# Self-attention on TensorE: a double unit from value products to scores, and new places for the projections

## The chip, the core and the metric

The kernel runs on one core of one Trainium2 chip. The metric is the time of one execution on the device, in microseconds; the median of several runs is compared. The core has TensorE (matmuls, transposes), ScalarE, VectorE, GpSimd and SyncE (starts DMAs). Each works through its own list of instructions in order, and they wait for each other by semaphores. The tables call them PE (its weight loads: PEld), ACT, DVE, POOL and SP.

## The reference, cut to what matters

After an adapter (a first attention over a short context) come a self-attention, a cross-attention and a feed-forward, each with a residual, for 4 batches of 512 tokens and 160 features. The change is in the self-attention:

```python
DIM, HEADS, DHEAD = (160, 20, 64)
def cross_attention(x, ctx, wq, wk, wv, wo, bo):          # here ctx is layer_norm(x) too
    q = jnp.einsum('bne,ef->bnf', x, wq).reshape(B, N, HEADS, DHEAD).transpose(0, 2, 1, 3)
    ...
    scores = jnp.einsum('bhnd,bhmd->bhnm', q, k) * SCALE
    attn = jax.nn.softmax(scores, axis=-1)
    out = jnp.einsum('bhnm,bhmd->bhnd', attn, v)
    out = out.transpose(0, 2, 1, 3).reshape(B, N, HEADS * DHEAD)
    return jnp.einsum('bnf,fe->bne', out, wo) + bo
x = cross_attention(layer_norm(x, g1, be1), layer_norm(x, g1, be1), wq1, wk1, wv1, wo1, bo1) + x
```

## The kernel before

The 20 heads are taken as 10 pairs (`j`), and a pair as 4 units (`u = 4j + q`): the scores of 128 tokens against all 512, for both heads. A batch has `NU` = 40 units. The loop over a batch is written out over `d` from 0 to 19, a *double unit* each (units `2d` and `2d + 1`); the loop over batches is a hardware loop for the first three, and a last body without a next batch. What is ahead of the current batch's end is taken from the next batch by `over`.

What is done for a pair or unit, with the letters used here:

- **Q, K, V** (`project`): the projections of pair `j`, all into one PSUM bank, `b_proj`. ScalarE copies or rounds the bank; for q and k VectorE then writes the rest (value minus rounded value), L558 and L562. The bank is free for the next projection after that; for V after ScalarE's copy, L486. Scores use q and k as rounded part and rest.
- **S** (`scores`, L380): scores of two units, each into its own pair of banks. Then for each unit VectorE takes the negated maxima (L566), ScalarE two exponentials with sums (L494), VectorE the reciprocals (L570, `inverses`), and GpSimd scales the probabilities in place (L633).
- **T** (`turns`, L394): eight transposes of one unit's probabilities into the two banks `b_turn`, one for each head. VectorE copies the first bank (L575), ScalarE the second (L505). A T waits for the copies of the T before it.
- **W** (`pv`, L407): value products of two units, from the copies and v. After a pair's last one ScalarE copies the result (`copy_att`, L500).

The scores run `LEAD` = 2 double units ahead: d begins with the scores of units `2d + 4` and `2d + 5`. Then follow W of units `2d - 2` and `2d - 1`, T(2d), a projection, T(2d + 1), and in even d one more. So TensorE's order is S W T V T Q in even d and S W T K T in odd d; V, Q and K of d are for pair `d // 2 + 2`.

Between these lies the layer norm of the next batch, or of the next block: statistics (L131, L135) at the end of d = 6 and standardizing at the end of d = 7 on VectorE (`LN_AT`), transposes into `b_proj` at the end of d = 11 and 13 (`TURN_MAIN`, `TURN_TAIL`; L157, L164), and from d = 15 (`ROUND_AT`) the rounding on ScalarE (L193 to L196) and the remainders on VectorE (L206, L208). At a batch's end TensorE does the last W and the output projection (L414) into `b_turn`, VectorE adds it to x (L583), and the loop jumps back.

## Time and profile before

| | |
|---|---|
| median of 3 runs | 1208.08 us (1207.51 to 1211.06) |
| profiled execution, its own time | 1205.71 us |
| its span, first to last instruction | 1203.6 us |
| TensorE busy | 1105.7 us, 92% of the span |
| VectorE, ScalarE, GpSimd busy | 57%, 54%, 29% |
| self-attention | about 213 to 886 us of the span |
| mean granted TensorE clock | 0.982 of full speed |

In a timeline a row begins with the start (us from the span's start) and the duration; [0.60 <-DVE ...] is the time that the engine was idle before, and what ended it. A matmul's shown end includes its drain, so a next matmul starts before it; a TensorE gap is therefore read between starts.

### The profile page before, as it was taken

What the parts mean: (1) busy time and instruction counts of PE and PEld (TensorE: products, weight loads), DVE (VectorE), ACT (ScalarE), POOL (GpSimd) and SP (SyncE); (2) the same over time, 40 slices, a digit from 0 to 9 for tenths busy, and PEclk for the clock granted to TensorE, in tenths of its full rate; (3) what the DMA queues carried; (4) which work ended last, traced back from release to release, by engine and by line L of the source; (5) the groups of instructions that cost most, each with busy time, mean ns of one, the idle gap of its engine ahead of it and who ended that gap; (6) DMA issues with size and microseconds to landing.
All of it is one profiled execution on the core that took longest, in us unless ns stands there. A gap on an engine that the chain in (4) does not pass through costs nothing. (4 is left out here: it accounts for less than half of the span.)

```text
span 1203.6 us, 20434 instructions
## 1 busy us (share of the span) xinstructions
PE 1105.7 (92%) x6668; PEld 759.2 (63%) x6668; DVE 684.5 (57%) x1350; ACT 654.6 (54%) x1450; POOL 352.9 (29%) x470
## 2 busy tenths in 40 slices
PE   7999999699999899998999998999889999999898
PEld 3555555465656665656656567656477878786787
DVE  4474564456665466563666644666547575757253
ACT  2543445366676366673666764666616464646242
POOL 2330322234433234331344322343313132312110
PEclk9999999699999999999999999999999999999899
DMA  6400000000000000000000000000120000000000
GB/s 180 103 1 1 0 1 1 0 1 2 1 1 2 2 1 1 1 1 3 1 1 1 1 1 1 1 1 1 39 55 2 1 0 0 0 1 1 1 22 23
DMA packets 17815, 13.69 MB, mean 11 GB/s; under 512 B 8196, under 2 KB 16324, under 8 KB 17732
## 3 DMA queue, kind: packets, MB, share of 16 engines
q1 hardware_dynamic: 17732, 12.60, 4.2%
q8 instruction: 50, 0.82, 0.3%
q14 instruction: 33, 0.27, 0.1%
HBM read 11.29 MB, written 1.31 MB: 10 GB/s over the span
## 5 line engine op out<-in xcount | busy, mean ns | idle before, releaser
L633 POOL TENSOR_SCALAR sa_probs<-sa_probs,sa_inverse 128x512 f32<-128x512 f32 x320 | 220.2, 701 | 408.4 <-DVE sa_inverse L570 408.4
L494 ACT ACTIVATE sa_probs<-banks,sa_negmax 128x512 f32<-128x512 f32 x320 | 217.5, 687 | 131.6 <-DVE sa_negmax L566 131.5
L566 DVE TENSOR_REDUCE sa_negmax<-banks 128x2 f32<-128x1024 f32 x160 | 194.3, 1217 | 83.7 <-PE banks L380 83.2
L394 PEld LDWEIGHTS banks<-ident,sa_probs 128*128 128x128 f32 x1280 | 144.1, 142 | 101.7 <-POOL sa_probs L633 52.7
L394 PE MATMUL banks<-ident,sa_probs 128*128 128x128 f32 x1280 | 173.5, 279 | 29.3 <-POOL sa_probs L633 26.5
L575 DVE COPY sa_turned<-banks 128x512 f32<-128x512 f32 x160 | 110.3, 689 | 89.5 <-PE banks L394 84.8
L380 PE MATMUL banks<-sa_k_parts,sa_q_parts 64*128 64x512 f32 x960 | 135.2, 412 | 22.9 <-DVE sa_k_parts L562 17.2
L407 PE MATMUL banks<-sa_turned,sa_v 128*64 128x512 f32 x640 | 155.2, 605 | 0.1
L505 ACT COPY sa_turned<-banks 128x512 f32<-128x512 f32 x160 | 94.4, 590 | 80.5 <-PE banks L394 80.5
L380 PEld LDWEIGHTS banks<-sa_k_parts,sa_q_parts 64*128 64x128 f32 x960 | 86.3, 187 | 61.3 <-ACT sa_probs L494 21.2
L1503 POOL TENSOR_TENSOR ca_probs<-ca_probs,ca_inverse 128x616 f32<-128x616 f32 x40 | 48.8, 1219 | 159.8 <-DVE ca_inverse L1451 159.8
L407 PEld LDWEIGHTS banks<-sa_turned,sa_v 128*64 128x64 f32 x640 | 38.6, 136 | 74.6 <-issue 72.4
L1383 ACT COPY ca_turned<-banks 77x512 f32<-77x512 f32 x80 | 42.7, 583 | 71.7 <-PE banks L1316 71.7
L1307 PEld LDWEIGHTS banks<-ca_k_diag,ca_q 128*128 128x128 f32 x320 | 44.4, 193 | 34.7 <-DVE ca_v L1432 23.3
L494 ACT ACTIVATION_READ_ACCUMULATOR sa_probs<-banks,sa_negmax 128x1 f32 x320 | 64.4, 201 | 0.0
L1307 PE MATMUL banks<-ca_k_diag,ca_q 128*128 128x154 f32 x320 | 53.1, 310 | 5.6 <-DVE ca_v L1432 3.1
L562 DVE TENSOR_TENSOR sa_k_parts<-banks,sa_k_parts 128x512 fp32r<-128x512 f32 x40 | 27.7, 692 | 49.6 <-ACT sa_k_parts L482 49.6
L1326 PE MATMUL banks<-ca_turned,ca_v 77*64 77x512 f32 x160 | 46.2, 634 | 2.3 <-ACT ca_turned L1383 2.3
L1336 PEld LDWEIGHTS banks<-w_o,ca_att 128*128 128x128 f32 x320 | 45.7, 198 | 4.0 <-issue 4.0
L1336 PE MATMUL banks<-w_o,ca_att 128*128 128x160 f32 x320 | 46.7, 309 | 0.0
L414 PEld LDWEIGHTS banks<-w_o,sa_att 128*128 128x128 f32 x320 | 43.6, 190 | 3.2 <-issue 3.2
L414 PE MATMUL banks<-w_o,sa_att 128*128 128x160 f32 x320 | 44.5, 300 | 0.0
(187 smaller groups left out, 1900.4 us busy)
## 6 DMA issues: line engine op xcount, KB each, us to landing
w_o<-in_L_xattn_wo SPq DMA_DIRECT2D x2, 800.0 KB, 6.7
out<-x SPq DMA_DIRECT2D x4, 320.0 KB, 2.4
x<-in_x SPq DMA_DIRECT2D x1, 960.0 KB, 5.7
ad_raw_main<-in_L_xattn_wq SPq DMA_DIRECT2D x1, 640.0 KB, 4.3
ad_raw_main<-in_L_xattn_wk SPq DMA_DIRECT2D x1, 640.0 KB, 6.3
ad_raw_main<-in_L_xattn_wv SPq DMA_DIRECT2D x1, 640.0 KB, 8.3
raw_main<-in_L_xattn_wq SPq DMA_DIRECT2D x1, 640.0 KB, 4.4
raw_main<-in_L_xattn_w_ff SPq DMA_DIRECT2D x1, 640.0 KB, 4.6
```

The source lines that it names most:

```text
L380: last = pe.matmul(bank[:, e, :], q_parts[rows, j % 2, a, q * P:(q + 1) * P], k_parts[rows, j % 2, c, :], start=(i == 0), stop=(i == 2))
L394: last = pe.transpose(b_turn[e][:, q * P:(q + 1) * P], probs[:, j % 2, e, q, k * P:(k + 1) * P], ident[:])
L407: last = pe.matmul(b_out[e * HD:(e + 1) * HD, :], v[:, V_BUF[j // 2], k, c:c + HD], turned[:, u % 2, e, :], start=(k == 0), stop=(k == QT ...
L414: last = pe.matmul(b_turn[q // 2][:, q % 2 * D:(q % 2 + 1) * D], att[:, j, q * P:(q + 1) * P], w_o[:, j, :], start=(j == 0), stop=(j == NP ...
L494: act.activation(probs[:, j % 2, e, q, :], b_scores[u % 2][:, e, :], ACT.Exp, bias=negmax[:, u % RING, e:e + 1], accum_out=total[:, u % RI ...
L505: act.copy(turned[:, u % 2, 1, :], b_turn[1]).then_inc(s_evac_act.sem, 1)
L566: dve.tensor_reduce(negmax[:, u % RING, :], b_scores[u % 2], AX_X, ALU.max, negate=True).then_inc(s_max.sem, 1)
L575: dve.tensor_copy(turned[:, u % 2, 0, :], b_turn[0]).then_inc(s_evac.sem, 1)
L633: pool.tensor_scalar(probs[:, j % 2, e, q, :], probs[:, j % 2, e, q, :], inverse[:, u % RING, e:e + 1], 1.0, ALU.mult, ALU.mult).then_inc( ...
L1307: last = pe.matmul(b_scores[:, q // 2, (q % 2) * 2 * SK:(q % 2 + 1) * 2 * SK], q_sb[:, j % BUFS, q * P:(q + 1) * P], k_diag[:, j % BUFS, : ...
L1336: last = pe.matmul(b_out[half][:, t * D:(t + 1) * D], att[:, j, q * P:(q + 1) * P], w_o[:, j, :], start=(j == 0), stop=(j == NPAIR - 1))
L1503: pool.tensor_tensor(p, p, inverse[:, j % BUFS, :].unsqueeze(2).broadcast_to([P, 2 * QT, SK]), ALU.mult).then_inc(s_norm.sem, 1)
```

## The change

TensorE's double unit now begins with the value products W and ends with scores, those of units `2d + 6` and `2d + 7` (the third next double unit). The projections have new places: V between W and T(2d) and K between the two T in even d, both for pair `d // 2 + 2`; Q between the two T in odd d, for pair `d // 2 + 3`. V's bank is copied by VectorE instead of ScalarE. ScalarE does both units' exponentials ahead of its copies of T. VectorE takes both maxima first, and issues the reciprocals of the double unit's second unit in the same double unit. The norm's transposes stand between W and T(2d), their scaling between the exponentials; its rounding and remainders stand at the head of d = 15. Ahead of the loop, Q and K of pairs 0 and 1 go into four banks (`b_proj`, `b_out`, `b_turn[0]`, `b_turn[1]`), V of the two follows behind the first scores, and the scores of six units (0 to 5) instead of four are made there, with Q of pair 2.

```diff
@@ TensorE
-            for what in (V, Q, K):
-                project(0, 0, what)
+            ln.ready(pe, 0)
+            project_q(0, 0, b_proj)
+            project_k(0, 0, b_out)
+            project_q(0, 1, b_turn[0])
+            project_k(0, 1, b_turn[1])
             scores(0, 0)
             scores(0, 1)
-            project(0, 1, V)
-            project(0, 1, Q)
-            scores(0, 2)
-            project(0, 1, K)
-            scores(0, 3)
+            project_v(0, 0, b_proj)
+            pe.wait_ge(s_klo.sem, s_klo.at(0, 0))
+            project_v(0, 1, b_out)
+            for u in range(2, 2 * LEAD):
+                scores(0, u)
+            project_q(0, 2, b_turn[0])
+            for u in range(2 * LEAD, 2 * LEAD + 2):
+                scores(0, u)
+            pe.wait_ge(s_qlo.sem, s_qlo.at(0, 2))
 
             def batch(b, more):
                 for d in range(ND):
                     norm, _, nb = following(b, more)
-                    for i in range(2):
-                        over(scores, b, 2 * (d + LEAD) + i, NU, more)
                     if d >= 1:
                         pv(b, 2 * d - 2)
                         pv(b, 2 * d - 1)
-                    turns(b, 2 * d)
...
+                    if d % 2 == 0:
+                        over(next_v, b, d // 2 + 2, NPAIR, more)
                     if d == TURN_MAIN:
                         norm.turn_main(pe, nb, ident, b_proj, lambda: pe.wait_ge(s_klo.sem, s_klo.at(b, d // 2 + 2)))
                     if d == TURN_TAIL:
                         norm.turn_tail(pe, nb, ident, b_proj, lambda: pe.wait_ge(s_klo.sem, s_klo.at(b, d // 2 + 2)))
+                    turns(b, 2 * d)
...
+                    if d % 2 == 0:
+                        over(next_k, b, d // 2 + 2, NPAIR, more)
+                    else:
+                        over(next_q, b, d // 2 + 3, NPAIR, more)
+                    turns(b, 2 * d + 1)
+                    for i in range(2):
+                        over(scores, b, 2 * (d + LEAD + 1) + i, NU, more)
@@ ScalarE
+                    if d == ROUND_AT:
+                        norm.round(act, nb, operands_free(b + 1))
                     over(exps, b, 2 * (d + LEAD), NU, more)
-                    if d % 2 == 0 and d > 0:
-                        copy_att(b, d // 2 - 1)
-                    copy_turned(b, 2 * d)
-                    if d < ND - 1:
-                        over(round_part, b, middle(d)[0], NPAIR, more, middle(d)[1])
-                    over(exps, b, 2 * (d + LEAD) + 1, NU, more)
-                    copy_turned(b, 2 * d + 1)
...
+                    over(exps, b, 2 * (d + LEAD) + 1, NU, more)
+                    if d % 2 == 0 and d > 0:
+                        copy_att(b, d // 2 - 1)
+                    copy_turned(b, 2 * d)
+                    if d % 2 == 0:
+                        over(round_k, b, d // 2 + 2, NPAIR, more)
+                    else:
+                        over(round_q, b, d // 2 + 3, NPAIR, more)
+                    copy_turned(b, 2 * d + 1)
@@ VectorE
+            def copy_v(b, j, bank=b_proj):
+                dve.wait_ge(s_v.sem, s_v.at(b, j))
+                dve.wait_ge(s_pv.sem, s_pv.at(b, 2 * QT * (V_BEFORE[j // 2] + 1) - 1))
+                dve.tensor_copy(v[:, V_BUF[j // 2], j % 2 * 2:j % 2 * 2 + 2, :].rearrange("p a c -> p (a c)"), bank).then_inc(s_vsb.sem, 1)
...
                     over(maxima, b, m, NU, more)
-                    over(inverses, b, m - 1, NU, more)
-                    if d % 2 == 1:
-                        over(rest, b, end(d - 1)[0], NPAIR, more, Q)
-                    if d == ROUND_AT + 1:
+                    if d == ROUND_AT:
                         norm.remainder(dve, nb, operands_free(b + 1))
                     over(maxima, b, m + 1, NU, more)
                     over(inverses, b, m, NU, more)
+                    if d % 2 == 0:
+                        over(copy_v, b, d // 2 + 2, NPAIR, more)
                     copy_turned(b, 2 * d)
-                    if d % 2 == 1 and d < ND - 1:
-                        over(rest, b, middle(d)[0], NPAIR, more, K)
+                    over(inverses, b, m + 1, NU, more)
                     copy_turned(b, 2 * d + 1)
...
+                    if d % 2 == 0:
+                        over(rest_k, b, d // 2 + 2, NPAIR, more)
+                    else:
+                        over(rest_q, b, d // 2 + 3, NPAIR, more)
```

TensorE in d = 2, before. L380 is S (one row for each of its two units), L407 the value products, L394 T, L226 to L229 the first of V's two identical fours, L218 the first of Q's four.

```order
L380 MATMUL banks<-sa_k_parts,sa_q_parts 128x512 x6
...
L380 MATMUL banks<-sa_k_parts,sa_q_parts 128x512 x6
L407 MATMUL banks<-sa_turned,sa_v 64x512 x2
...
L407 MATMUL banks<-sa_turned,sa_v 64x512 x2
L394 MATMUL banks<-ident,sa_probs 128x128 x8
L226 MATMUL banks<-wc_hi,ln_y_hi 128x256
...
L394 MATMUL banks<-ident,sa_probs 128x128 x8
...
L218 MATMUL banks<-ln_y_hi,wa_hi 128x512
```

TensorE in d = 2 with the change. L410 is the value products, L397 T, L383 S, and L218 with the weights `wb_hi` is K.

```order
L410 MATMUL banks<-sa_turned,sa_v 64x512 x2
...
L410 MATMUL banks<-sa_turned,sa_v 64x512 x2
...
L226 MATMUL banks<-wc_hi,ln_y_hi 128x256
...
L397 MATMUL banks<-ident,sa_probs 128x128 x8
L218 MATMUL banks<-ln_y_hi,wb_hi 128x512
...
L397 MATMUL banks<-ident,sa_probs 128x128 x8
...
L383 MATMUL banks<-sa_k_parts,sa_q_parts 128x512 x6
...
L383 MATMUL banks<-sa_k_parts,sa_q_parts 128x512 x6
```

V has moved ahead of the first T, K stands where V or Q stood, and the scores are at the end.

VectorE in d = 2 and the head of d = 3, before: maxima L566, reciprocals L570, copies of T L575, the rest of q L558.

```order
L566 TENSOR_REDUCE sa_negmax<-banks 128x2
...
L570 RECIPROCAL sa_inverse<-sa_total 128x2
...
L566 TENSOR_REDUCE sa_negmax<-banks 128x2
...
L570 RECIPROCAL sa_inverse<-sa_total 128x2
...
L575 COPY sa_turned<-banks 128x512
...
L575 COPY sa_turned<-banks 128x512
...
L566 TENSOR_REDUCE sa_negmax<-banks 128x2
...
L570 RECIPROCAL sa_inverse<-sa_total 128x2
...
L558 SCALAR_TENSOR_TENSOR sa_q_parts<-banks,sa_q_parts 128x512
```

VectorE in d = 2 with the change: maxima L575, reciprocals L579, V's copy L571, copies of T L584, the rest of k L566.

```order
L575 TENSOR_REDUCE sa_negmax<-banks 128x2
...
L575 TENSOR_REDUCE sa_negmax<-banks 128x2
...
L579 RECIPROCAL sa_inverse<-sa_total 128x2
...
L571 COPY sa_v<-banks 128x512
...
L584 COPY sa_turned<-banks 128x512
...
L579 RECIPROCAL sa_inverse<-sa_total 128x2
...
L584 COPY sa_turned<-banks 128x512
L566 TENSOR_TENSOR sa_k_parts<-banks,sa_k_parts 128x512
```

The second reciprocal now stands between the two copies instead of behind the next maximum, V's copy has come in, and the rest of k ends the double unit.

ScalarE in d = 3, before: exponentials L494 (two a unit), copies of T L505, k's rounding L482.

```order
L494 ACTIVATE sa_probs,sa_total<-banks,sa_negmax 128x512 x2
...
L505 COPY sa_turned<-banks 128x512
L482 CAST sa_k_parts<-banks 128x512
L494 ACTIVATE sa_probs,sa_total<-banks,sa_negmax 128x512 x2
...
L505 COPY sa_turned<-banks 128x512
```

ScalarE in d = 3 with the change: exponentials L500, copies of T L511, q's rounding L488.

```order
L500 ACTIVATE sa_probs,sa_total<-banks,sa_negmax 128x512 x2
...
L500 ACTIVATE sa_probs,sa_total<-banks,sa_negmax 128x512 x2
...
L511 COPY sa_turned<-banks 128x512
...
L488 ACTIVATE sa_q_parts<-banks 128x512
...
L511 COPY sa_turned<-banks 128x512
```

The first copy of T has moved behind the second unit's exponentials.

## Rows read from the trace of the kernel before

**Rows 1.** TensorE's waits, 245 to 886 us: total us, times, longest.

```profile
PE banks L394 <- POOL sa_probs L633: 25.4, 38, 2.4
PE banks L380 <- DVE sa_k_parts L562: 15.8, 27, 0.6
...
PE banks L157 <- DVE sa_k_parts L562: 2.5, 4, 0.6
PE banks L164 <- DVE sa_k_parts L562: 2.1, 4, 0.5
```

**Rows 2.** Timeline of TensorE, an even and an odd double unit.

```profile
269.62 1.09 PE L394 MATMUL banks<-ident,sa_probs 128*128 128x128 f32 x8 [0.38 <-POOL sa_probs L633]
270.46 0.36 PE L226 MATMUL banks<-wc_hi,ln_y_hi 128*128 128x256 f32 x1
...
272.34 0.50 PE L218 MATMUL banks<-ln_y_hi,wa_hi 128*128 128x512 f32 x1
...
273.47 1.65 PE L380 MATMUL banks<-sa_k_parts,sa_q_parts 64*128 64x512 f32 x12
275.05 1.94 PE L407 MATMUL banks<-sa_turned,sa_v 128*64 128x512 f32 x8
276.92 1.09 PE L394 MATMUL banks<-ident,sa_probs 128*128 128x128 f32 x8
...
278.78 1.04 PE L394 MATMUL banks<-ident,sa_probs 128*128 128x128 f32 x8
280.42 1.66 PE L380 MATMUL banks<-sa_k_parts,sa_q_parts 64*128 64x512 f32 x12 [0.60 <-DVE sa_k_parts L562]
```

**Rows 3.** Timeline of TensorE, end of a batch and start of the next.

```profile
383.82 1.09 PE L394 MATMUL banks<-ident,sa_probs 128*128 128x128 f32 x8 [0.43 <-DVE sa_turned L575]
...
400.47 1.66 PE L380 MATMUL banks<-sa_k_parts,sa_q_parts 64*128 64x512 f32 x12 [1.69 <-issue]
404.56 1.09 PE L394 MATMUL banks<-ident,sa_probs 128*128 128x128 f32 x8 [2.43 <-POOL sa_probs L633]
...
409.91 1.65 PE L380 MATMUL banks<-sa_k_parts,sa_q_parts 64*128 64x512 f32 x12
```

**Rows 4.** Timelines of VectorE and ScalarE in the stretch of rows 2.

```profile
274.47 1.22 DVE L566 TENSOR_REDUCE sa_negmax<-banks 128x2 f32<-128x1024 f32 x1 [1.55 <-PE banks L380]
...
277.70 0.69 DVE L575 COPY sa_turned<-banks 128x512 f32<-128x512 f32 x1
279.60 0.69 DVE L562 TENSOR_TENSOR sa_k_parts<-banks,sa_k_parts 128x512 fp32r<-128x512 f32 x1 [1.20 <-ACT sa_k_parts L482]
...
271.70 0.59 ACT L486 COPY sa_v<-banks 128x512 f32<-128x512 f32 x1 [0.29 <-PE banks L229]
...
275.73 0.69 ACT L494 ACTIVATE sa_probs<-banks,sa_negmax 128x512 f32<-128x512 f32 x1 [1.12 <-DVE sa_negmax L566]
...
278.98 0.59 ACT L482 CAST sa_k_parts<-banks 128x512 fp32r<-128x512 f32 x1 [0.27 <-PE banks L221]
279.46 0.69 ACT L494 ACTIVATE sa_probs<-banks,sa_negmax 128x512 f32<-128x512 f32 x1
...
280.80 0.59 ACT L505 COPY sa_turned<-banks 128x512 f32<-128x512 f32 x1
```

**Rows 5.** Timeline of VectorE: statistics and next maximum, a remainder.

```profile
287.55 1.00 DVE L131 BATCH_NORM_STATS2 ln_stats<-x 128x6 f32 x4
...
289.19 1.23 DVE L566 TENSOR_REDUCE sa_negmax<-banks 128x2 f32<-128x1024 f32 x1
...
358.48 1.06 DVE L208 TENSOR_TENSOR ln_y_tail<-ln_full_tail,ln_y_tail 32x512 fp32r<-32x512 f32 x1
```

**Rows 6.** Stretches: length, busy (instructions) of each engine, clock, DMA.

```profile
213.38:245.63 32.25, 24.80 (x109) 16.83 (x109) 12.45 (x18) 14.05 (x34) 7.10 (x11) 0.68 0.00 1
...
399.00:410.00 11.00, 7.10 (x42) 6.09 (x42) 4.41 (x7) 4.44 (x11) 2.71 (x4) 0.84 0.01 1
238.00:242.00 4.00, 3.26 (x17) 3.27 (x18) 1.64 (x3) 1.03 (x3) 1.87 (x3) 0.57 0.00 0
```

More of the change, by code:

```diff
@@ L353, in _, with project_q, project_k, project_v @@
                 pe.sem_inc(s.sem, s.credit)
-            def project(b, j, what):
-                if what == V:
-                    if j == 0:
-                        ln.ready(pe, b)
-                    pe.wait_ge(s_klo.sem, s_klo.at(b, j - 1))
-                    for t in range(2):
-                        last = ln.project_tokens(pe, b_proj[:, t * 2 * P:(t + 1) * 2 * P], w_v, j // 2 * 2 * P, j % 2 * 2 + t, 2 * P)
-                    last.then_inc(s_v.sem, 1)
-                elif what == Q:
-                    pe.wait_ge(s_vsb.sem, s_vsb.at(b, j))
-                    ln.project(pe, b_proj, w_q, j * P).then_inc(s_q.sem, 1)
-                else:
-                    pe.wait_ge(s_qlo.sem, s_qlo.at(b, j))
-                    ln.project(pe, b_proj, w_k, j * P).then_inc(s_k.sem, 1)
+            def project_q(b, j, bank=b_proj):
+                ln.project(pe, bank, w_q, j * P).then_inc(s_q.sem, 1)
+            def project_k(b, j, bank=b_proj):
+                ln.project(pe, bank, w_k, j * P).then_inc(s_k.sem, 1)
+            def project_v(b, j, bank=b_proj):
+                for t in range(2):
+                    last = ln.project_tokens(pe, bank[:, t * 2 * P:(t + 1) * 2 * P], w_v, j // 2 * 2 * P, j % 2 * 2 + t, 2 * P)
+                last.then_inc(s_v.sem, 1)
+            def next_q(b, j):
+                if j == 0:
+                    ln.ready(pe, b)
+                pe.wait_ge(s_klo.sem, s_klo.at(b, j - 1))
+                project_q(b, j)
+            def next_v(b, j):
+                pe.wait_ge(s_qlo.sem, s_qlo.at(b, j))
+                project_v(b, j)
+            def next_k(b, j):
+                pe.wait_ge(s_vsb.sem, s_vsb.at(b, j))
+                project_k(b, j)
             def scores(b, u):
@@ L466, in _ @@
         def _(act):
-            for s in (s_vsb, s_exp, s_att, s_evac_act):
+            for s in (s_exp, s_att, s_evac_act):
                 act.sem_inc(s.sem, s.credit)
@@ L642, in _ @@
             add_bias(0)
-            for u in range(2 * LEAD - 1):
+            for u in range(2 * LEAD):
                 scale(0, u)
@@ L648, in batch @@
                     m = 2 * (d + LEAD)
-                    over(scale, b, m - 1, NU, more)
                     over(scale, b, m, NU, more)
+                    over(scale, b, m + 1, NU, more)
                     if d == LN_AT:
```

86 lines of the change are left out of this document (33 added, 53 removed).

## The prediction

> **What bounds the kernel now.** I went from the coarse view to the fine one. The busy shares of the page name the engine that sets the end (TensorE 92%, the next 57%), and the table of waits says what it waits for: little, and regularly. From 245 to 886 us it waits 38 times for GpSimd's scaled probabilities (25.4 us in all) and 27 + 4 + 4 = 35 times for VectorE's second half of k (15.8 + 2.5 + 2.1 us) [rows 1]. Waits on the other engines cost nothing while TensorE has work.
>
> The timeline of TensorE shows one even and one odd double unit [rows 2]. Reading starts against starts (matmuls drain under the next one's start), the pieces cost: S, the scores of two units, 273.47 to 275.05 = 1.58; W, the value products of two units, 275.05 to 276.92 = 1.87; T, the transposes of one unit, 269.62 to 270.46 = 0.84; V and T 270.46 to 272.34, so V 1.04; Q 272.34 to 273.47 = 1.13; K with the T ahead of it 276.92 to 278.78 = 1.86, so K 1.01. Two double units hold 2 S, 2 W, 4 T, V, Q, K = 13.5 us. The time that they take is longer by two gaps: S at 280.42 starts 0.80 after the T ahead of it is issued (278.78 + 0.84 = 279.62), shown as 0.60 idle because 0.20 is drain, and T at 269.62 starts 0.43 late (0.38 idle).
>
> Why these two? K stands in the odd double unit with only one T (0.84) between it and the S that needs it, while ScalarE must round K and VectorE subtract: K starts at 276.92 + 0.84 = 277.76, ScalarE 1.22 later at 278.98 for 0.59, VectorE at 279.60 for 0.69 [rows 4]. T waits for GpSimd since VectorE's reciprocal of the last unit is issued only behind the next double unit's first maximum.
>
> **The change, part by part.** The cyclic order on TensorE was S W T V T Q, S W T K T; it becomes S W V T K T, S W T Q T. S written at the end of d is the S that stood at the head of d + 1, so scores do not come earlier. What moves is Q and K, each to the double unit before, V by one T, and the reciprocal of the second unit.
>
> *Removed.* K now has S, W, T, Q, T (6.3 us) between it and its first S, against a chain of 1.22 + 0.59 + 0.69 = 2.5: the 35 waits go, 20.4 idle + 35 x 0.20 drain = 27.4 us. The reciprocal now stands behind the copy of T's first half in the same double unit; GpSimd has over 5 us until the T in question, where it now has 3: the GpSimd waits go, except that three of the 38 are batch starts of 2.43 [rows 3]. 25.4 - 7.3 = 18.1 idle over 35 places, 0.05 each of drain more, 19.8. In the last double unit of batches 0 to 2 two T stand back to back and the second starts 0.43 + 0.25 of drain late [rows 3]; Q now stands between: 3 x 0.68 = 2.0. Together 49.2 us.
>
> *Added, ordinary units.* I wrote the new cycle down from S's start at 0 with the offsets of [rows 4]: first maximum 1.00 after S; exponentials 1.26 after the maximum; two exponentials take 1.34 of ScalarE; its copies 0.48 when back to back; T start to VectorE's copy of the first half 0.78, ScalarE's of the second half 0.42 later, half a T; V start to its copy 1.24; a semaphore adds some 0.06. In the even unit V starts at 3.45, VectorE's copy (now there, 0.69 as its other passes over a bank take, where ScalarE took 0.59) runs 4.69 to 5.38, K may start at 5.44, and TensorE is ready at 3.45 + 1.04 + 0.84 = 5.33. So a wait of 0.1 in 34 places, 3.4 us; none, were the copy as quick as on ScalarE. The Trainium skill, "VectorE: DVE Perf Modes", errata section, gives 120 + 512 cycles at 0.96 GHz for such a copy; the estimate is 0.66 us, with which the sum would be 1 us smaller. The row's 0.69 is used.
>
> The second T starts at 6.45 and the unit ends at 7.29. VectorE copies that T from 7.23, then writes the rest of k to 8.46, while the maximum of the next S could start at 7.29 + 1.00: it starts at 1.16 after that S. In the odd unit the exponentials then run 2.41 to 5.09, and only then comes ScalarE's copy of T's second half, which stood ahead of the second exponential before. It is done at 5.74; TensorE reaches that half of the second T at 3.45 + 0.84 + 1.13 + 0.42 = 5.84. Covered, by 0.1. This is the thinnest cover of the change; without it each 0.1 costs 0.1 in some 38 places. In even units it is 0.5.
>
> *Added, units with more work.* Here the same chain is late. Statistics at the end of d = 6 hold VectorE 1.64 us [rows 5], now behind the rest of k: the maximum of d = 7 starts at 8.46 + 1.64 - 7.29 = 2.8, exponentials end at 6.73, ScalarE's copy at 7.38, and the second T ends at 7.80 instead of 6.27: 1.5. The four standardizing steps at the end of d = 7 leave d = 8 just covered, as no T is late there. Norm transposes at d = 11 and 13 stand between W and T, their scaling between the two exponentials: 0.37 each, 0.7. The rounding at d = 15 goes ahead of the exponentials (three copies, some 0.6 each as those in [rows 4]) and the remainders (a full one of 0.69 and one of 1.06) between the maxima [rows 5]: second T ends 7.76 instead of 6.27, 1.5. These are 3.7 in each of batches 0 to 2. In the last batch no projection fills d = 15, so 2.6 there, and 0.3 in each of d = 16 and 17: 5.5. With the 3.4 above: 3 x 3.7 + 5.5 + 3.4 = 20.0. Bounds: nothing, if ScalarE keeps up; and 40, if every cover is 0.5 thinner than worked out.
>
> *Batch starts.* Now S at 400.47 is followed by 2.5 us of waiting [rows 3]. Afterwards V and T come first (1.9 us), but K waits for V's copy, which VectorE issues behind both maxima of d = 0, and these start only after the update of x and VectorE's own loop jump. TensorE ends at 400.47 - 1.69 = 398.78; the update takes some 0.5 more (an estimate: 320 elements, against the 512 in 0.69) and the same jump 1.7, so the maximum is at 401.1, or 0.6 counted from V; exponentials at 1.9, reciprocal 3.4, copy to 4.1, K 4.2 against 1.9. A wait of 2.3 takes the place of 2.5: 3 x 0.2 = 0.6 gained, no more. The bounds are 0 and the whole 7.5.
>
> *Start.* From the first V to the first W, 213.38 to 245.63, TensorE is idle 32.25 - 24.80 = 7.45 us [rows 6]: every part waits for the one bank's last reader. On four banks Q, K, Q, K run on; I find 1.5 left at the sixth score unit, waiting for ScalarE's four units in a row, and 1.0 at K(2) waiting for V's copy: 5.0 gained. K(2) is moved in, not added. The granted clock was 0.68 over it, and 0.57 from 238 to 242, so mostly at the lower of its two levels (1.2 GHz), behind waits for the first exponentials. That stretch has 3.26 us busy, 1.9 at full speed: 1.4 lost. I count them as gained, as those waits go; the slow stretch ahead stays. Together 6.4; bounds 3 and 9.
>
> At the batch starts the clock is 0.84 in 399 to 410 [rows 6]: from the T at 404.56 to the S at 409.91 are 5.35 us, where 2 T, V and Q need 3.85, so 1.5 is lost [rows 3]. The Trainium skill, "TensorE: Matmul & The Clock Gate", Part 1, says that idleness halves the clock and sustained work restores it, and the rows agree. By it the stretch stays slow after the change, as 1.7 and 2.3 us of idle around 1.9 of work remain; were it to run at the upper level, 3 x 1.5 = 4.5 us more would be gained. I count none.
>
> *Sum.* -49.2 + 20.0 - 0.6 - 6.4 = -36.2 on the profiled execution's 1205.71 (span 1203.6, 2.1 outside it): 1169.5. The median shown is 2.4 above it, so 1171.9, rounded 1172. The change adds no DMA; SyncE's loads of the next weights wait for the last Q, which comes one double unit sooner.
>
> **Rivals.** First, the wait moves to a copy: ScalarE's copy behind two exponentials is 0.4 later than I have it, or K waits for V as long as S waited for K. For it: covers of 0.1. Against it: lateness does not build up, since a late T shifts S, copies and maxima together. Price: 0.3 to 0.4 x 38 = 11 to 15 us, or 34 x 0.7 = 24; the time is 1183 to 1200. Chance 0.17.
>
> Second, other side: the same mechanism at odd and even units alike. ScalarE's copy late by L costs (L - 0.1) x 38 + (L - 0.5) x 36; at L = 0.8 that is 26.6 + 10.8, the whole gain. It decides from exponentials that start 3.2 after S instead of 2.4 on, as in a chain where VectorE's rest and copy run after every T and hold the next maximum. Time 1209 to 1225; chance 0.05. Against it: VectorE has four maxima of 1.2 and seven passes of 0.69, 9.7 us of work in 13.5.
>
> Third, the units with more work hide theirs, and the batch starts lose their wait: 49.2 + 6.4 + 7.5 - 8 = 55, 1153. Chance 0.06. Fourth, the moves exchange waits one for one, no change beyond 0.3%, 3.6 us, about what a measurement can tell: 0.03. Mine, 1160 to 1183, has the remaining 0.69.
>
> **The numbers.** 1172 is the likeliest case. With the first rival's nearer part the range is 1159 to 1187; the upper part of the first rival, the second and the third lie outside, about 0.2. Faster 0.92, same 0.03, slower 0.05.
>
> **What would show it.** In the profile after: no wait of the scores' line for the rest of k; GpSimd waits of the transposes' line below 2 us; a regular cycle of two double units of 13.6 instead of 14.7; K's first matmul with 0.1 idle; a wait of transposes for ScalarE's copy in d = 7, 11, 13, 15, some 1.5 at the most; at the batch starts K behind V's copy, about 2.3; the first W near 239. Wrong would be an even or odd unit with a wait of over 0.3 every time.

## The result and the profile after

The changed kernel takes 1177.8 us in the median of 4 runs (1172.6 to 1182.6) beside 1207.8 of the kernel before (4 runs too, where the table ahead has 3): a ratio of 0.975, interval 0.970 to 0.980. Measured again on another chip, it took 1175.2 (first experiment), ratio 0.972 (0.969 to 0.976). Forecast were 1172, with 1159 to 1187. The profiled execution took 1172.6 with a span of 1170.6 us.

The page of the changed kernel shows TensorE busy about as long as before (1109.2 us against 1105.7), in a span that is 33.0 us shorter. VectorE's share went up from 57% to 61%, with V's copies.

```profile
span 1170.6 us, 20482 instructions
PE 1109.2 (95%) x6668; PEld 760.1 (65%) x6668; DVE 712.3 (61%) x1390; ACT 637.6 (54%) x1410; POOL 350.0 (30%) x470
```

What TensorE waits for in the changed kernel, 245 to 860 us (total us, times, longest), the answer to [rows 1]:

```profile
PE banks L397 <- ACT sa_turned L511: 5.5, 17, 0.6
PE banks L397 <- DVE sa_turned L584: 4.4, 9, 1.0
PE banks L397 <- issue: 4.3, 2, 2.1
PE banks L218 <- DVE sa_v L571: 3.5, 3, 2.3
...
PE banks L226 <- issue: 2.2, 2, 1.2
```

The 45.8 us in which TensorE waited for the rest of k and for GpSimd are gone. In their place stand 9.9 us for copies of T, where the kernel before had 2.7, and 10.0 at the three batch starts (the rows with "issue" and V's copy L571).

TensorE of the changed kernel, an odd and an even double unit with full work, the answer to [rows 2]. Left out are the other matmuls of Q, V and K:

```profile
236.60 1.65 PE L383 MATMUL banks<-sa_k_parts,sa_q_parts 64*128 64x512 f32 x12
238.18 1.94 PE L410 MATMUL banks<-sa_turned,sa_v 128*64 128x512 f32 x8
240.05 1.09 PE L397 MATMUL banks<-ident,sa_probs 128*128 128x128 f32 x8
240.90 0.47 PE L218 MATMUL banks<-ln_y_hi,wa_hi 128*128 128x512 f32 x1
...
241.91 1.04 PE L397 MATMUL banks<-ident,sa_probs 128*128 128x128 f32 x8
242.87 1.65 PE L383 MATMUL banks<-sa_k_parts,sa_q_parts 64*128 64x512 f32 x12
...
246.32 0.39 PE L226 MATMUL banks<-wc_hi,ln_y_hi 128*128 128x256 f32 x1
...
247.38 1.04 PE L397 MATMUL banks<-ident,sa_probs 128*128 128x128 f32 x8
248.33 0.50 PE L218 MATMUL banks<-ln_y_hi,wb_hi 128*128 128x512 f32 x1
...
249.37 1.04 PE L397 MATMUL banks<-ident,sa_probs 128*128 128x128 f32 x8
250.33 0.96 PE L383 MATMUL banks<-sa_k_parts,sa_q_parts 64*128 64x512 f32 x6
```

From S at 236.60 to S at 250.33 are 13.73 us, with no idle shown. Read the starts more closely. T ahead of Q takes 240.90 - 240.05 = 0.85, but T ahead of S 242.87 - 241.91 = 0.96, and again 250.33 - 249.37 = 0.96, so going over to scores costs 0.11 that no row calls idle. And T ahead of K takes 0.95: this is the forecast 0.1 of waiting for V's copy, which ends just ahead of K's start at 248.33:

```profile
247.58 0.69 DVE L571 COPY sa_v<-banks 128x512 f32<-128x512 f32 x1 [0.80 <-PE banks L229]
```

The copy ended at 247.58 + 0.69 = 248.27.

A unit with more work, d = 7: VectorE, TensorE and ScalarE of the changed kernel.

```profile
278.90 0.99 DVE L131 BATCH_NORM_STATS2 ln_stats<-x 128x6 f32 x4
...
280.34 2.33 DVE L575 TENSOR_REDUCE sa_negmax<-banks 128x2 f32<-128x1024 f32 x2
...
281.39 1.09 PE L397 MATMUL banks<-ident,sa_probs 128*128 128x128 f32 x8
...
283.98 0.66 PE L397 MATMUL banks<-ident,sa_probs 128*128 128x128 f32 x4 [0.57 <-DVE sa_turned L584]
284.88 0.66 PE L397 MATMUL banks<-ident,sa_probs 128*128 128x128 f32 x4 [0.25 <-ACT sa_turned L511]
285.47 1.66 PE L383 MATMUL banks<-sa_k_parts,sa_q_parts 64*128 64x512 f32 x12
...
284.23 0.60 ACT L511 COPY sa_turned<-banks 128x512 f32<-128x512 f32 x1
```

The maxima start 2.4 after their S at 277.93 (1.0 in a unit without statistics), and the four exponentials follow. VectorE's copy of T at 283.23 holds the first half of the next T, which waits 0.57; ScalarE's copy comes last, at 284.23, and the second half waits 0.25 for it. From the first T to the next S are 4.08 us, against 2.82 at 240.05: 1.26 lost.

Start of a batch, TensorE and then VectorE of the changed kernel, behind a jump of the loop, the answer to [rows 3]:

```profile
387.23 0.38 PE L226 MATMUL banks<-wc_hi,ln_y_hi 128*128 128x256 f32 x1 [1.20 <-issue]
...
390.56 1.96 PE L397 MATMUL banks<-ident,sa_probs 128*128 128x128 f32 x8 [2.12 <-issue]
393.08 0.80 PE L218 MATMUL banks<-ln_y_hi,wb_hi 128*128 128x512 f32 x1 [0.56 <-DVE sa_v L571]
...
396.80 1.90 PE L383 MATMUL banks<-sa_k_parts,sa_q_parts 64*128 64x512 f32 x12
...
386.19 0.49 DVE L592 TENSOR_TENSOR x<-banks,x 128x320 f32 x1 [4.94 <-PE banks L417]
389.31 2.36 DVE L575 TENSOR_REDUCE sa_negmax<-banks 128x2 f32<-128x1024 f32 x2 [2.63 <-issue]
```

"Issue" means that nothing in the profile released the engine. Such idle time stands where an engine comes back from the jump: 1.20 ahead of V, 2.12 more between V and T, and 2.63 on VectorE between the update of x and the first maximum. T then runs at about half the clock, 1.96 where 1.09 is usual. At the second batch start the three stops are 1.04, 2.13 and 2.51. The last batch, whose start has no jump behind it, shows only the wait that was forecast:

```profile
711.02 0.51 PE L218 MATMUL banks<-ln_y_hi,wb_hi 128*128 128x512 f32 x1 [2.30 <-DVE sa_v L571]
```

### The profile page after: what moved, and what is told of

Same layout as the page of the kernel before. It is cut to its first block and busy times, and to the rows that moved or that the text cites. A ratio compares the mean times of both kernels' runs of the same rounds, so it can differ in the third digit from the quotient of the medians.

```text
span 1170.6 us, 20482 instructions
## 1 busy us (share of the span) xinstructions
PE 1109.2 (95%) x6668; PEld 760.1 (65%) x6668; DVE 712.3 (61%) x1390; ACT 637.6 (54%) x1410; POOL 350.0 (30%) x470
## 5 line engine op out<-in xcount | busy, mean ns | idle before, releaser
L646 POOL TENSOR_SCALAR sa_probs<-sa_probs,sa_inverse 128x512 f32<-128x512 f32 x320 | 217.1, 693 | 382.8 <-DVE sa_inverse L579 382.6
L500 ACT ACTIVATE sa_probs<-banks,sa_negmax 128x512 f32<-128x512 f32 x320 | 215.9, 685 | 167.2 <-DVE sa_negmax L575 154.8
L575 DVE TENSOR_REDUCE sa_negmax<-banks 128x2 f32<-128x1024 f32 x160 | 188.8, 1219 | 15.0 <-PE banks L383 8.9
L397 PE MATMUL banks<-ident,sa_probs 128*128 128x128 f32 x1280 | 177.2, 280 | 14.8 <-ACT sa_turned L511 5.5
L397 PEld LDWEIGHTS banks<-ident,sa_probs 128*128 128x128 f32 x1280 | 148.3, 143 | 61.6 <-issue 33.5
L584 DVE COPY sa_turned<-banks 128x512 f32<-128x512 f32 x160 | 110.2, 689 | 86.3 <-PE banks L397 86.1
L410 PE MATMUL banks<-sa_turned,sa_v 128*64 128x512 f32 x640 | 155.0, 605 | 0.0
L383 PE MATMUL banks<-sa_k_parts,sa_q_parts 64*128 64x512 f32 x960 | 133.8, 410 | 1.9 <-ACT sa_probs L500 1.9
L511 ACT COPY sa_turned<-banks 128x512 f32<-128x512 f32 x160 | 94.4, 590 | 34.2 <-PE banks L397 30.9
L383 PEld LDWEIGHTS banks<-sa_k_parts,sa_q_parts 64*128 64x128 f32 x960 | 84.4, 186 | 31.0 <-issue 14.6
L410 PEld LDWEIGHTS banks<-sa_turned,sa_v 128*64 128x64 f32 x640 | 38.7, 136 | 74.3 <-issue 73.7
L500 ACT ACTIVATION_READ_ACCUMULATOR sa_probs<-banks,sa_negmax 128x1 f32 x320 | 64.6, 202 | 0.0
L579 DVE RECIPROCAL sa_inverse<-sa_total 128x2 f32<-128x2 f32 x160 | 26.1, 163 | 47.2 <-ACT sa_probs L500 47.2
L218 PE MATMUL banks<-ln_y_hi,wa_hi 128*128 128x512 f32 x80 | 38.5, 481 | 7.3 <-issue 3.5
```

The lines of the kernel that those rows point to most:

```text
L383: last = pe.matmul(bank[:, e, :], q_parts[rows, j % 2, a, q * P:(q + 1) * P], k_parts[rows, j % 2, c, :], start=(i == 0), stop=(i == 2))
L397: last = pe.transpose(b_turn[e][:, q * P:(q + 1) * P], probs[:, j % 2, e, q, k * P:(k + 1) * P], ident[:])
L410: last = pe.matmul(b_out[e * HD:(e + 1) * HD, :], v[:, V_BUF[j // 2], k, c:c + HD], turned[:, u % 2, e, :], start=(k == 0), stop=(k == QT ...
L500: act.activation(probs[:, j % 2, e, q, :], b_scores[u % 2][:, e, :], ACT.Exp, bias=negmax[:, u % RING, e:e + 1], accum_out=total[:, u % RI ...
L511: act.copy(turned[:, u % 2, 1, :], b_turn[1]).then_inc(s_evac_act.sem, 1)
L575: dve.tensor_reduce(negmax[:, u % RING, :], b_scores[u % 2], AX_X, ALU.max, negate=True).then_inc(s_max.sem, 1)
```

## The experiments

The intervals of the ratio to the kernel before are some 0.4% to either side, 5 us. So each run is also read by the stages of its profiled execution, which TensorE's starts divide: *start*, from the first projection to the first W; *bodies*, from W in d = 1 to the output projection, one for each batch; *joints*, from the output projection to the next W in d = 1. The first two joints hold the jump of the loop, the third has none. In us:

```
                                start  bodies                        joints
before                          32.25  142.02 141.99 141.99 133.82   23.85 22.61 21.96
the change                      22.64  136.71 136.73 136.74 129.03   23.74 23.66 20.42
the change again                22.65  136.75 136.74 136.74 129.80   22.22 24.42 20.41
before, reciprocal early        32.17  137.78 137.71 137.81 130.38   20.92 20.55 19.19
the change, reciprocal late     22.06  137.22 137.16 137.18 129.45   24.75 25.71 21.01
the change, one-bank start      30.90  136.80 136.74 136.72 129.00   24.82 24.15 20.43
the change, V on ScalarE        23.52  138.33 138.31 138.30 131.30   21.66 20.09 21.23
the change, no loop             22.12  136.34 136.30 136.30 128.99   20.33 20.30 20.31
before, no loop                 32.33  141.52 141.55 141.49 134.07   21.95 21.94 21.95
the change, first V early       25.53  137.43 136.74 136.73 130.23   22.82 21.81 21.19
the change, T copied first      22.66  136.44 136.40 136.43 127.70   22.38 23.20 20.40
the change, load spread         22.64  135.08 135.11 135.09 127.19   23.01 24.09 18.86
load spread, no loop            22.30  134.54 134.57 134.52 127.18   18.73 20.25 18.72
the change, loop shifted        24.90  136.72 136.73 136.72 129.03   24.35 24.10 20.41
```

With the change a body of the first three batches holds one S (1.6) more than before and a joint 1.5 less; the start holds one K (1.0) more and the last body one less. Full bodies repeat to 0.1 us; joints and the parts outside self-attention vary by 1 to 4 us with the granted clock, as the change against its own repetition shows.

**The change again.** The same file on another chip: 1175.2 us (1170.6 to 1180.7).

> The changed kernel as it is, for the comparisons of this series. Its four executions lay between 1172.6 and 1182.6 us with mean clocks of 0.975 to 0.985; if the spread comes with the granted clock, the span follows the clock again: about 1172 at 0.985 and 1181 at 0.976.

The time follows the clock again: 1173.2 us at 0.985, and 1180.5 and 1180.7 at 0.977.

**Before with the second reciprocal early.** Which part of the change takes away the GpSimd waits? In the kernel before, only the reciprocals of the double unit's second unit move, from behind the next first maximum to the end of their own double unit:

```diff
+            inverses(0, 3)
...
                     over(maxima, b, m, NU, more)
-                    over(inverses, b, m - 1, NU, more)
...
                     copy_turned(b, 2 * d + 1)
+                    over(inverses, b, m + 1, NU, more)
```

> The kernel before, with one change: VectorE issues the reciprocals of a double unit's second unit at the end of that double unit instead of behind the next one's first maximum. If the wait of the transposes for GpSimd comes from that place, as the prediction has it, 19.8 us in 35 places go and the three waits of 2.43 at the batch starts too, perhaps with their slow clock: 1174 to 1179 us, ratio 0.973 to 0.978. The rival, that the waits only change their name (then the exponentials or the rest of k end last), gives no change: above 1200.

1182.3 us, ratio 0.980 (0.976 to 0.983). TensorE's waits, 215 to 890 us:

```profile
PE banks L380 <- DVE sa_k_parts L562: 16.6, 28, 1.4
PE banks L394 <- DVE sa_turned L575: 8.5, 14, 1.0
```

The k waits stay, those for GpSimd are gone. In self-attention this one line saves 24.0 us, the whole change 30.8. Of the 24.0, 16.1 are in the bodies; the joints are 2.1 to 2.9 shorter. The median is 3 above the range that was expected: the waits for VectorE's copy of T grew from 2.7 us to 8.5.

**The change with the reciprocal late.** The reverse: all of the change, with the reciprocals back behind the next first maximum.

```diff
-            inverses(0, 3)
...
                     over(maxima, b, m, NU, more)
+                    over(inverses, b, m - 1, NU, more)
...
-                    over(inverses, b, m + 1, NU, more)
```

> The changed kernel with the reciprocals back behind the next first maximum. Two theories of why the wait for GpSimd is gone. By the prediction's sentence the new place of the reciprocal removed it: then 20 us come back, about 1198. The other: V now stands between the value products and the transposes and gives GpSimd 1.04 us more, against a wait of 0.43: then at most 2 us come back, 1178 to 1180. By the offsets (reciprocal at 2.4 after S, GpSimd to 3.9, transposes at 4.5) I now expect the second.

1179.3 us, ratio 0.977 (0.973 to 0.980). TensorE's waits for GpSimd, 215 to 890 us:

```profile
PE banks L397 <- POOL sa_probs L645: 13.5, 5, 4.9
```

5 places instead of 38: the three batch starts (4.9, 4.9, 2.9) and two of 0.4. Bodies grow by only 0.4 to 0.5. So the edits overlap. W and V (1.87 + 1.04) now stand ahead of T(2d) and cover GpSimd's lateness by themselves.

**The change with a one-bank start.** Ahead of the loop all projections go into `b_proj` again, each behind the last reader of the one before; the order stays.

```diff
-            project_q(0, 0, b_proj)
-            project_k(0, 0, b_out)
-            project_q(0, 1, b_turn[0])
-            project_k(0, 1, b_turn[1])
+            project_q(0, 0)
+            pe.wait_ge(s_qlo.sem, s_qlo.at(0, 0))
+            project_k(0, 0)
+            pe.wait_ge(s_klo.sem, s_klo.at(0, 0))
+            project_q(0, 1)
...
```

> The changed kernel, with the first projections all in one bank, each waiting for the last reader of the one before. The prediction counted 6.4 us for the four banks, the profile of the changed kernel shows 9.6 us less between the first projection and the first value product. 6 to 10 us come back, 1184 to 1188 us, and the clock from 215 to 235 us is near 0.5 again; if the new order alone made the start quicker, nothing comes back.

1186.3 us, ratio 0.982 (0.978 to 0.986). The start is 8.3 longer than with four banks and the bodies are the same. So the banks are 8.3 of the start's gain of 10.6 (9.6, and the added K), the order the rest. The granted clock from 215 to 235 us is 0.66, with four banks 0.91:

```profile
215.73:246.63 30.90, 23.31 (x112) 15.50 (x112) 15.77 (x24) 12.86 (x32) 8.45 (x13) 0.78 0.00 1
```

Of the 8.3, 5.0 are idle time and 3.3 busy time at the lower clock: 30.90 - 23.31 = 7.59 idle here, 2.62 with four banks.

**The change with V copied by ScalarE.** `copy_v` moves to ScalarE, behind the second exponentials.

```diff
@@ ScalarE
                     over(exps, b, 2 * (d + LEAD) + 1, NU, more)
+                    if d % 2 == 0:
+                        over(copy_v, b, d // 2 + 2, NPAIR, more)
...
@@ VectorE
-                    if d % 2 == 0:
-                        over(copy_v, b, d // 2 + 2, NPAIR, more)
```

> The changed kernel with V's copy back on ScalarE, behind the second exponentials. Then the copy cannot start before ScalarE has done both units' exponentials, at 5.1 after S, and ends at 5.7, where K could start at 5.3: 0.3 to 0.4 in some 36 places instead of 0.1, so 8 to 12 us slower than the change, 1183 to 1187. If the prediction's offsets are wrong and ScalarE has room there, nothing changes; if it becomes the bound, the loss is above 20.

1180.1 us, ratio 0.979 (0.975 to 0.983). The bodies are 1.6 longer, the last 2.3. V on VectorE is worth some 7 us in the bodies. The median is below the 1183 to 1187 that were expected, since the two joints with a jump are 2.1 and 3.6 shorter. That is not ScalarE's copy being early: at the joint without a jump K waits 3.31 for it instead of 2.30, and the joint is 0.8 longer. What is gone is VectorE's stop (and the second joint keeps the upper clock level). Its first maximum follows the update of x at once, at the first joint and in the same way at the second:

```profile
394.26 0.49 DVE L596 TENSOR_TENSOR x<-banks,x 128x320 f32 x1 [4.94 <-PE banks L417]
394.79 2.35 DVE L579 TENSOR_REDUCE sa_negmax<-banks 128x2 f32<-128x1024 f32 x2
```

So VectorE jumps here too and does not stop. What in its code decides that no run isolates; this one takes ten copies a batch out of its list.

**The change and the kernel before without the loop.** The four batches of self-attention are written out; order and work are the same.

```diff
+def each_batch(eng, body):
+
+    for b in range(B):
+        body(b, b < B - 1)
...
-            over_batches(pe, batch)
+            each_batch(pe, batch)
...
```

> The changed kernel with the four batches of self-attention written out, no jump back. In the change's trace the two starts with a jump have 1.1 and then 2.1 us on TensorE and 2.6 on VectorE in which nothing is waited for that the profile shows; the start of the last batch, without a jump, has none, and is 3.2 us shorter. If the jump is what costs, both go: 6.5 us less, 1168 to 1170, and what stays is K's wait of 2.3 for V's copy. The rival: those gaps belong to the order (transposes waiting for x's update or probabilities); then nothing changes.

> The kernel before, written out in the same way. There the scores come first behind the jump and a wait of 2.4 for GpSimd follows, which hides most of what the jump delays on the other engines. So by the theory that the change laid the jump bare, only 1 to 3 us are gained, 1205 to 1207; if a jump costs 3.3 us wherever it stands, 6 to 7.

The change without the loop: 1164.6 us, ratio 0.967 (0.963 to 0.971); before without it: 1201.3, ratio 0.995 (0.992 to 0.998). All joints of each kernel become alike, 20.3 and 21.9. So the two jumps cost the changed kernel 3.4 each, (23.74 - 20.33) + (23.66 - 20.30) = 6.8, and the kernel before 1.9 and 0.7, 2.6. Both medians are some 4 us below what was expected. Without the jump, TensorE and VectorE of the changed kernel:

```profile
382.72 0.39 PE L232 MATMUL banks<-wc_hi,ln_y_hi 128*128 128x256 f32 x1
...
383.78 1.04 PE L403 MATMUL banks<-ident,sa_probs 128*128 128x128 f32 x8
386.99 0.77 PE L224 MATMUL banks<-ln_y_hi,wb_hi 128*128 128x512 f32 x1 [2.17 <-DVE sa_v L577]
...
383.44 2.35 DVE L581 TENSOR_REDUCE sa_negmax<-banks 128x2 f32<-128x1024 f32 x2
```

Self-attention is 8.7 shorter in the changed kernel and 3.7 in the kernel before. The rest of the 11 to 13 between the changed kernel's medians goes with the clock, 0.987 on average in those executions, and 0.980 and 0.983 in the change's two series; the rest of the kernel before's 7 lies within its interval (2 to 10 us). T stands right behind V, the maxima right behind the update of x (383.03), and the wait of K for V's copy is what the prediction said.

**The change with the first V early.** At d = 0 VectorE copies V ahead of both maxima.

```diff
+                    if d == 0:
+                        over(copy_v, b, d // 2 + 2, NPAIR, more)
                     over(maxima, b, m, NU, more)
```

> The changed kernel, with V's copy of the first double unit of a batch ahead of the two maxima on VectorE. If K's wait at the batch starts (2.3 at the last, 0.6 behind a late T at the others) comes from that place in VectorE's order, it goes, with the slow clock behind it: 3 to 7 us less, 1168 to 1172. If the exponentials of d = 0, which then start 0.7 later, end last, nothing is gained.

1175.5 us, ratio 0.975 (0.972 to 0.979), no gain. K no longer waits, but the maxima come 0.6 later, and at the first batch the second T waits for its copy instead:

```profile
234.93 0.66 PE L397 MATMUL banks<-ident,sa_probs 128*128 128x128 f32 x4 [2.05 <-DVE sa_turned L584]
```

The start grows by 2.9, the joint without a jump by 0.8; those with one shrink by 0.9 and 1.9.

**The change with T copied first.** ScalarE's copy of T(2d) ahead of the second exponentials, in every d.

```diff
-                    over(exps, b, 2 * (d + LEAD) + 1, NU, more)
...
                     copy_turned(b, 2 * d)
+                    over(exps, b, 2 * (d + LEAD) + 1, NU, more)
```

> In every double unit of self-attention ScalarE copies its half of the second unit's turned probabilities before it takes the second unit's exponentials of the next scores, not behind them. First theory, by the prediction's thin cover of 0.1 us per double unit and by the trace of the changed kernel, where TensorE's transposes and value products wait 5.5 us in all (17 times) for this copy: 2 to 5 us less than the changed kernel, 1170 to 1175. Rival: the exponentials come 0.3 to 0.6 us later and the scores that need their bank then wait, in up to 63 double units: 10 us or more slower than the changed kernel.

1172.5 us, ratio 0.972 (0.968 to 0.976). The 17 waits for ScalarE's copy are gone, those for VectorE's grew from 4.4 to 8.6. Bodies are 0.3 shorter, the last 1.3: 2.2 us, as the first theory said. The ordinary units had next to nothing to give.

**The change with the load spread.** The statistics divided over d = 3 and 5, and ScalarE's copy of T first in the units with more work alone.

```diff
@@ ScalarE
+                    busy = d in (7, TURN_MAIN, TURN_TAIL, ROUND_AT)
+                    if busy:
+                        copy_turned(b, 2 * d)
                     over(exps, b, 2 * (d + LEAD) + 1, NU, more)
...
@@ VectorE
-                    if d == LN_AT:
-                        norm.statistics(dve, nb)
+                    if d == LN_AT - 3:
+                        norm.statistics(dve, nb, (0, 1))
+                    if d == LN_AT - 1:
+                        norm.statistics(dve, nb, (2, 3))
```

> Two edits for the double units that carry more work than the rest: the next stage's row statistics, all of which VectorE takes in one double unit (d = 6), are divided over d = 3 and d = 5, and in d = 7, 11, 13 and 15 ScalarE copies the second unit's turned probabilities ahead of the exponentials. First theory: the changed kernel pays 3.7 us per full batch there, as predicted, and gets back most of it: some 8 to 12 us less than the changed kernel, 1165 to 1169. Rival: the waits that the trace of the changed kernel lists there are only some 2 us per batch and the statistics themselves are still in VectorE's way wherever they stand: 2 to 5 us less, 1171 to 1175.

1169.2 us, ratio 0.968 (0.964 to 0.972). Bodies are 1.6 shorter and the last 1.8: 6.7 us, between the two expectations. The two edits were not run apart. The unit d = 7 is ordinary now, 286.81 - 280.52 = 6.29 from S to S:

```profile
280.52 1.66 PE L385 MATMUL banks<-sa_k_parts,sa_q_parts 64*128 64x512 f32 x12
...
285.85 1.04 PE L399 MATMUL banks<-ident,sa_probs 128*128 128x128 f32 x8
286.81 1.66 PE L385 MATMUL banks<-sa_k_parts,sa_q_parts 64*128 64x512 f32 x12
```

**Load spread, and no loop.**

> The version with spread load, and the four batches of self-attention written out in place of a loop of the program (as in the run without the loop, 1164.6). The two gains lie at different places (inside the batches, and at the two joints with a jump), so they should add up: by the first theory 1154 to 1158, by the rival 1160 to 1164.

1157.5 us (1155.2 to 1159.8), ratio 0.959 (0.955 to 0.963): the fastest version, some 18 to 20 us under the change. Self-attention takes 624.8 us instead of 643.6. The gains of the bodies (load) and joints (jump) add up.

**The change with the loop shifted.** 47 more waits on TensorE ahead of the loop, for a value long reached, move the jump's target.

```diff
-            pe.wait_ge(s_qlo.sem, s_qlo.at(0, 2))
+            for _ in range(48):
+                pe.wait_ge(s_qlo.sem, s_qlo.at(0, 2))
```

> The changed kernel with 47 more waits on TensorE ahead of the loop, on a semaphore value long reached, so that they cost their issue once (1 to 3 us in the start stage) and shift the loop's first instruction by 47 places. In the changed kernel four packets of instructions are moved between 384 and 392 us, at the first joint, and none in the version without the loop; one of them stands at about 389.8, just ahead of the T that starts at 390.56 behind 2.12 of idle. First theory: instructions are fetched in blocks, the block at the jump's target ends within V, and the next one is fetched only then; moved by 47 places, V and T lie in one block, the 2.12 goes at both joints with a jump and they come to 21.4 to 22.2 us, with 1.2 to 2 of idle left ahead of V. Rival: TensorE stops between V and T for another reason (a semaphore or a register that the profile does not name), and the joints stay at 22 to 24.5 with the same 2.1.

1179.5 us, ratio 0.978 (0.975 to 0.980): 2 to 4 above the change, 2.3 of it in the start. The first joint, TensorE and VectorE:

```profile
387.64 0.38 PE L226 MATMUL banks<-wc_hi,ln_y_hi 128*128 128x256 f32 x1 [1.29 <-issue]
...
388.69 1.04 PE L397 MATMUL banks<-ident,sa_probs 128*128 128x128 f32 x8
393.31 0.80 PE L218 MATMUL banks<-ln_y_hi,wb_hi 128*128 128x512 f32 x1 [3.58 <-DVE sa_v L572]
...
386.51 0.49 DVE L593 TENSOR_TENSOR x<-banks,x 128x320 f32 x1 [4.94 <-PE banks L417]
389.54 2.35 DVE L576 TENSOR_REDUCE sa_negmax<-banks 128x2 f32<-128x1024 f32 x2 [2.53 <-issue]
```

The 2.12 between V and T are gone, as the first theory said: they came from where the code lies. The rival's reason for them is refuted. But the joints are no shorter, as only the rival said, and that is VectorE's doing: its first maximum still comes 2.53 behind the update, V's copy is as late as before, and K waits 3.58 instead of 0.56. TensorE's second stop had been hidden behind VectorE's.

The DMA traffic fits. Between 384 and 392 us the changed kernel moves these packets of instructions, by two queues, and the version without the loop none in the eight microseconds around its joint, 380 to 388:

```profile
q8 instruction: 2, 0.03, 1.7%
q14 instruction: 2, 0.02, 0.8%
```

The Trainium skill, "Runtime: NRT & Kernel Launch", section "Instruction fetch mechanics", says that code streams in ahead of its use in blocks of 16 KiB, and that a taken branch out of the loaded blocks stalls the engine until the target's block has come. The trace agrees for queue q8: 0.82 MB in 50 packets over the span is that size for each. The packets of q14 are half as large, 0.34 MB in 42. The price of the stops is from the rows.

The times of the packets suggest which engine stops for which. Those of q8 start at 384.6 and 387.8, both 2.7 us ahead of an end of TensorE's idle time (V at 387.23, T at 390.56). A packet of q14 starts at 387.3, between VectorE's update and its first maximum, and the next at 389.8. In the kernel before, where VectorE is ready when S is, and in the version with V on ScalarE, where it doesn't stop, q14 moves nothing at the first joint:

```profile
q8 instruction: 2, 0.03, 1.6%
q8 instruction: 2, 0.03, 1.2%
```

These are all the packets from 396 to 406 us of the kernel before, and from 391 to 401 of the one with V on ScalarE. That q8 carries TensorE's code and q14 VectorE's is my reading; no row names the engine. With it, VectorE's stop is not a price of every jump but, like TensorE's second stop, one of where its code lies.

## Why the prediction was right, and where it was not

The prediction's profiled sum was 1169.5 us and 1172.6 came out: of the 36.2 us forecast, 33.1. Part of that closeness is luck: the bodies gave 4.8 and the joints 4.4 less than forecast, the start 4.2 more, and 2.3 came from outside self-attention. By terms, from the table of stages:

*Removed waits and their size.* Both sorts of waits went, and none but K's 0.1 took their place in ordinary units. But the bodies gained less than forecast. With the contents made equal they are 5.3 + 1.6 = 6.9 shorter in each full batch and 4.8 - 1.0 = 3.8 in the last, 24.4; forecast were 49.2 - 20.0 = 29.2. Of the 4.8 missing, 35 x 0.12 = 4.2 lie in the step that priced the k wait at 0.60 idle and 0.20 drain. That took T ahead of S as 0.84, as it is ahead of K. [rows 2] already held the better figure, since Q ahead of S took 1.13 where a projection ahead of T takes 1.0: S starts 0.11 to 0.12 late behind anything. A removed k wait was worth 0.68. So the cycle is 13.73 and not 13.6. (K's cover was a T larger than the prediction listed, T, S, W, T, Q, T, some 7.1 us; that changed nothing.)

*Which edit removes the GpSimd wait.* The prediction gave it to the reciprocal. That is enough, as the second experiment shows, but not necessary: with the reciprocal late, V's new place does it too. The step was incomplete, at no cost to the sum.

*Added, ordinary units.* K's 0.1 behind V's copy is there, in the starts and not as idle. With ScalarE's copy, "none, were the copy as quick as on ScalarE", the bodies grew by 1.6: it is not its duration that counts but the queue of four exponentials that it stands behind. The thin cover of 0.1 for ScalarE's copy of T held: copying it first gave 0.3 per body, though the prediction saw 38 places at risk.

*Added, units with more work.* Forecast 3.7 per batch, measured 3.7: 1.3 in d = 7 and 1.1 in d = 15 (forecast 1.5 each), 0.8 in d = 11 and 0.6 in d = 13 (0.37 each). Spreading the load got 1.6 of it back.

*Batch starts.* This step of the prediction failed. It had 2.3 of waiting in place of 2.5, 0.6 gained in all; with contents equal the joints changed by +1.4, +2.5 and -0.1, 3.8 lost. The step let VectorE's jump take as long as TensorE's, "the same jump 1.7". VectorE's rows say 2.63 and 2.51. The kernel before could not show that figure, and did not have it. Its first maximum stood behind the S of TensorE, 1.00 after the start at 400.47 [rows 3], and VectorE was ready by then:

```profile
401.47 1.23 DVE L566 TENSOR_REDUCE sa_negmax<-banks 128x2 f32<-128x1024 f32 x1 [2.03 <-PE banks L380]
```

A stop there was at most 2.03 long (2.23 at the second joint). With the change no S is at the head, VectorE's stop has come in, and it sets the joint. That is 0.9 + 0.8 = 1.7 of the 4.4 missing. The joint without a jump came out as forecast, 2.30. The other 2.7 I put down to the clock, without a run for it alone, so their cause stays open: from K at 393.08 to W at 398.63 are 5.55 us, for 3.6 at the upper level, 2.0 lost where [rows 3] lost 1.5; and the first two joints of kernels with the same head lie between 22.2 and 24.8. The runs without the loop give the price of the jumps directly: 6.8 us with the change against 2.6 before, 4.2 more. The forecast had nothing for that difference.

*Start.* Forecast 6.4, measured 9.6, and 10.6 with K(2) counted. The stretch is 22.64 long with 20.02 busy (the row of the stretch, with the granted clock as third number from the end):

```profile
215.54:238.18 22.64, 20.02 (x113) 14.27 (x113) 15.49 (x24) 12.88 (x32) 8.43 (x13) 0.92 0.00 1
```

Idle fell from 7.45 [rows 6] to 2.62, 4.8 for the forecast 5.0. The clock rose from 0.68 to 0.92, and busy time fell by 24.80 - 20.02 + 1.0 = 5.8, where the prediction counted 1.4: it took the stretch with the waits for exponentials alone and left "the slow stretch ahead". With four banks the projections run without gaps and are at the upper level from 219.96 on. The run with one bank has the lower clock back, and 3.3 us of busy time with it.

Together -36.2 + 4.8 + 4.4 - 4.2 = -31.2; self-attention measures -30.8. The rest to -33.1 lies outside the change: the adapter ran 2.2 later, the later stages took 4.4 less, with the clock of that execution.

*Rivals.* The first (the wait moves to a copy in ordinary units, 1183 or more) did not occur; the second needed exponentials that start 3.2 after S, and they start 2.3 after it (245.14 against 242.87). The third had the units with more work and the batch starts free of cost; the first cost what the prediction said and the second more. The fourth, no change, is excluded by the ratio of 0.975.

## What to carry to other kernels

A wait between two engines can often be removed from either side: by giving the late result earlier (here one reciprocal, 24 of 31 us) or by putting other work ahead of the reader. Try the one-line edit first, and don't add up two edits that cover the same wait. When matmuls are priced, read start to start for each pair of neighbours: what follows an instruction changes its cost, here by 0.11 us, and idle columns do not show it. And look at the jump of every engine before reordering a loop's head: what stands first there decides whose stop is hidden, and adding to an engine's list can bring a stop that was not there. Writing the loop out saved 11 to 13 us here.

## What the hardware showed beyond that

A jump of the loop can stop each engine by itself. TensorE stood idle for 1.0 to 1.9 us at every jump of these runs. VectorE stood idle for 2.5 to 2.8 in most versions of the change, for 3.2 and 3.3 with the reciprocal late, and not at all with V's copies on ScalarE. In most versions of the change TensorE stopped once more between V and T, for 1.8 to 2.7 us, and by the reading above that is where the next block of code begins soon behind the target. Shifting the code by 47 instructions removed that second stop, and put a stop of 1.82 into the start, ahead of the loop's first V.

TensorE's clock makes up most of the spread between executions. Of the changed kernel, executions with a mean granted clock of 0.985 and 0.984 took 1172.6 and 1174.9 us, those with 0.977 and 0.975 took 1182.6 and 1180.8. Behind a stop the fall comes late: behind the jump, V at 387.23 still runs at the upper level and T at 390.56 at the lower one, and in the kernel before the T behind 2.43 of idle still took 1.09 [rows 3]. The same first projections of self-attention took the upper level at their beginning in one execution and the lower in another (first matmul 0.47 and 0.76 us, both behind 3.46 of idle).
